# The maximum stage of an attention kernel: two heads a load in 16-row transfers, whole query blocks as units in two 2-bank buffers

## The chip, the cores and the metric

The program runs on one core of one Trainium2 chip. The metric is the time of one execution in device microseconds. A core has five engines that work side by side and meet at semaphores: the tensor engine (PE, with PEld for its weight loads), VectorE (DVE), ScalarE (ACT), GpSimd (POOL) and SyncE (SP), which here only issues DMAs. PSUM, where products land, has 8 banks of 512 fp32 columns on each of 128 partitions.

## The reference

Input x is (4, 2048, 256), H = 16 heads of dh = 16. The output is x plus a causal attention plus a gated layer with 4-bit quantised operands, both on the normalised x:

```python
xn = layernorm(x)
qkv = xn @ Wqkv.T
q, k, v = split into heads of 16
dots = einsum('bhid,bhjd->bhij', q, k) * dh ** -0.5
dots = where(causal_mask, -inf, dots)
attn = softmax(dots)
out = x + (attn @ v) @ Wout.T + bout + fp4_gated_layer(xn)
```

## The kernel before

Four stages follow each other. The weights are prepared; then x is normalised and projected, and q and k go to DRAM, each as a sum of `PARTS` = 3 bf16 parts (`dram["q"]`, `dram["k"]`, a row of T = 2048 tokens for each part and dimension). Then comes the *maximum stage*, `shift_phase`, which this change is about: it finds for each query the largest allowed score, so that the main stage can subtract it before the exponential. The main stage computes the scores again, the probabilities, the values and the gated layer.

The maximum stage goes through B = 4 batches and 2 rounds of `MAX_HEADS` = 8 heads each, so 8 rounds and 64 heads. It needs only maxima, so it folds the keys in halves: of 128 keys, the first 64 (call their scores a) and the next 64 (b). The larger of both is a + relu(b - a). The tensor engine computes b - a into `DIFF` with one product, whose operands stack q parts and their negatives (`q_diff`) on parts of k shifted by 64 tokens and unshifted (`k_st`), and a into `S` with a second product of `q_st` on the same `k_st`. ScalarE writes relu(`DIFF`) to `excess` (line 730). VectorE adds `S` and `excess` and reduces over the columns with a maximum (line 751, one instruction that runs as a reduction and a short read of the accumulator). At the diagonal, a second small product of an identity and `future` adds -1e30 where keys lie ahead (line 686).

A *unit* is one query block i of 128 rows with up to `MAX_KEYS` = 1024 of its (i + 1) x 128 keys, so up to 512 folded columns: 24 units a head, 10 of them with 512 columns and two each with 64, 128, ... 448. Blocks 8 to 15 have two units; the second writes `second_max`, joined with `row_max` at the round's end (line 755). The order pairs a large unit with a small one. `DIFF` and `S` have `MAX_BUFS` = 4 buffers of one bank each, `excess` has 8.

The order on the tensor engine is written out: for each unit u of the round first the differences of u + `MAX_LEAD` (2), then the scores of u. Differences wait until ScalarE has read the unit that had the buffer 4 before, scores until VectorE has reduced the unit 4 before. At a head's first unit, the differences also wait for its load (`stack_ld`) and for GpSimd (`q_negated`), which makes the negative q rows from those that were loaded to `q_st` (line 639).

The loads have two buffers, for even and odd heads. SP waits until VectorE signals at the last unit of a head that its stacks are free (`stack_free`, line 750), and issues the head after next: 8 DMAs of `load_head` (line 547). `MAX_Q` and `MAX_K` give each DMA a first row and the parts it brings. Two parts, or one part twice, are one DMA of 2 x 16 rows with the 2 as its outermost dimension.

At a round's end the tensor engine turns the 128 x 128 maxima (line 719) into the last `DIFF` buffer, ScalarE and VectorE make two bf16 parts of it (lines 734, 758), and GpSimd stores them. The next round's product into that buffer waits for `part1`.

Of the kernel before, what the change touches and what calls it, by code (L numbers as in the profile page):

```python
# [14 lines left out]
P = 128  # L15
# [523 lines left out]
def load_head(eng, dst, src, runs, h, first, tokens, sem):  # L539

    for row, parts in runs:
        n = len(parts)
        if parts[0] == parts[-1]:
            rows = src[parts[0], bass.ds(h * DH, DH), bass.ds(first, tokens)].unsqueeze(0).to_broadcast([n, DH, tokens])
        else:
            rows = src[parts[0]:parts[-1] + 1, bass.ds(h * DH, DH), bass.ds(first, tokens)]
        eng.dma_start(dst[row:row + n * DH, 0:tokens], rows).then_inc(sem, 16)


MAX_KEYS = 1024  # L550
MAX_BUFS = 4
MAX_EXCESS = 8
MAX_LEAD = 2
# [3 lines left out]
def max_units():  # L557

    units = []
    for i in range(NKB):  # L560
        for k0 in range(0, (i + 1) * P, MAX_KEYS):
            units.append((i, k0, min(MAX_KEYS, (i + 1) * P - k0), k0 > 0))
    units.sort(key=lambda unit: -unit[2])
    half = len(units) // 2
    return [unit for pair in zip(units[:half], units[:half - 1:-1]) for unit in pair]


def shift_phase(nc, once, loop_sems, ident, dram):
# [9 lines left out]
    split = MAX_KEYS // P  # L578
    primed = []
    sem = loop_sems(primed)  # L580
    with ExitStack() as ctx:
# [11 lines left out]
        row_max, second_max = sb("m_row_max", [P, MAX_HEADS, NKB]), sb("m_second_max", [P, MAX_HEADS, NKB - split])  # L593
# [9 lines left out]
        joined, turned, part0, part1, stored, shift_st = (  # L603
            sem("m_joined"), sem("m_turned"), sem("m_part0"), sem("m_part1"), sem("m_stored"), once("m_st"))
        aside = once("m_aside")
        rounds = H // MAX_HEADS
        per_round = MAX_HEADS // 2
        head_dmas = len(MAX_Q) + 2 * len(MAX_K)
# [4 lines left out]
        def heads_before(n, h):  # L613

            return n * per_round + h // 2

        round_units = [(h, *unit) for h in range(MAX_HEADS) for unit in units]

        def uses(n, u, bufs):

            return n * (len(round_units) // bufs) + u // bufs + 1

        @block.gpsimd
        def _(pool):
# [10 lines left out]
            def negate(n, h):  # L635
                p = h % 2
                pool.wait_ge(q_ld[p], heads_before(n, h) * (16 * len(MAX_Q)) + 16 * len(MAX_Q) + PRIMED)
                pool.wait_ge(stack_free[p], heads_before(n, h) + PRIMED)
                pool.tensor_tensor(q_diff[p][rows, :], zero[rows, 0:1].to_broadcast([MAX_ROWS, T]), q_st[p][rows, :],  # L639
                                   ALU.subtract).then_inc(q_negated[p], 1)  # L640
# [10 lines left out]
            for h in range(2):  # L651
                negate(0, h)
            with pool.Fori(0, B * rounds - 1) as n:
                for h in range(2, MAX_HEADS):
                    negate(n, h)
                for h in range(2):
                    negate(n + 1, h)
                store(n)
            for h in range(2, MAX_HEADS):
                negate(B * rounds - 1, h)  # L660
            store(B * rounds - 1)

        @block.sync
        def _(sp):
            with sp.Fori(0, B) as b:
                with sp.Fori(0, rounds) as r:
                    n = b * rounds + r
                    for h in range(MAX_HEADS):
                        p = h % 2
                        sp.wait_ge(zeroed[p], 3)  # L670
                        sp.wait_ge(stack_free[p], heads_before(n, h) + PRIMED)
                        head = r * MAX_HEADS + h
                        load_head(sp, q_st[p][MAX_SECOND:P, :], dram["q"], MAX_Q, head, b * T, T, q_ld[p])
                        load_head(sp, q_diff[p], dram["q"], MAX_Q, head, b * T, T, stack_ld[p])

                        load_head(sp, k_st[p], dram["k"], MAX_K, head, b * T + PAIR, T - PAIR, stack_ld[p])
                        load_head(sp, k_st[p][MAX_SECOND:P, :], dram["k"], MAX_K, head, b * T, T, stack_ld[p])

        @block.tensor
        def _(pe):  # L680
            def product(out, q, h, i, k0, keys, mask):

                of = k_st[h % 2][:, k0:k0 + 2 * keys].rearrange("r (n k) -> r n k", k=P)[:, :, 0:PAIR]
                ins = pe.matmul(out[:, 0:keys], q[:, i * P:(i + 1) * P], of, start=True, stop=mask is None)  # L684
                if mask is not None:
                    ins = pe.matmul(out[:, keys - PAIR:keys], ident_bf[:, :], mask, start=False, stop=True)  # L686
                return ins

            def differences(n, u):
                h, i, k0, keys, _ = round_units[u]  # L690
                if u % len(units) == 0:
# [16 lines left out]
            with pe.Fori(0, B) as b:  # L708
                with pe.Fori(0, rounds) as r:
# [3 lines left out]
                    for u in range(len(round_units)):  # L713
                        if u + MAX_LEAD < len(round_units):
                            differences(n, u + MAX_LEAD)
# [679 lines left out]
```

## Time and profile before

| | |
|---|---|
| median of 3 runs | 3051.47 us (3048.34 to 3060.48) |
| profiled execution, first to last instruction | 3047.1 us |
| busy: PE, DVE, ACT, POOL | 2621.8, 1949.4, 2030.3, 694.1 us |
| maximum stage, first product to last part | 251.47 to about 1257 us |
| granted clock, share of DMA engines busy, 250 to 500 us | 0.83, 0.18 |
| VectorE busy, ScalarE busy, 250 to 500 us | 181.03, 159.65 us |

Times are microseconds of one profiled execution, counted from its first instruction. Durations overlap at their ends, because engines are pipelined: a product's record holds the time until its last column has landed. PEclk is the granted tensor clock as a share of 2.4 GHz. DMA share is the mean busy share of 16 DMA engines. "[4.31 <-DMA m_k<-s_k]" reads: the engine stood still for 4.31 us, and this transfer ended it; "issue" is rest that nothing in the profile accounts for.

### The profile page before, as it was taken

The numbers are of one execution on the slowest core, as the hardware profiler recorded it, in microseconds if no ns is written. First come the engines' busy times: TensorE is split into PE (matmuls) and PEld (weight loads), VectorE is DVE, ScalarE is ACT, GpSimd is POOL, SyncE is SP. The second block draws the span as 40 slices with busy tenths as digits, with TensorE's granted clock in tenths as the row PEclk, the third lists the DMA queues.
The fourth block names the chain that finished last, engine by engine and source line by source line (L and its number), as shares of the span: only waits on it lengthen the run. The fifth ranks groups of instructions, "written<-read, shape, count | busy, mean of one in ns | idle before, by whom it ended". The sixth has DMA issues, their size and how long they took to land.

```text
span 3047.1 us, 60898 instructions
## 1 busy us (share of the span) xinstructions
PE 2621.8 (86%) x18236; PEld 1350.3 (44%) x18236; DVE 1949.4 (64%) x5533; ACT 2030.3 (67%) x3510; POOL 694.1 (23%) x510
## 2 busy tenths in 40 slices
PE   2995777777777777599999999999999999999999
PEld 2872333333333333244444544444544444544445
DVE  6986677776777767455656456665556565555665
ACT  1655566665666666387777577777577777677775
POOL 3652212222122222221121121121122111111121
PEclk9997788887888888799999999999999999999999
DMA  2772211121111121322023122113212203302200
GB/s 74 256 255 59 55 47 50 51 53 53 47 50 50 53 53 48 80 43 43 22 37 75 46 37 47 35 28 66 61 28 42 43 22 63 73 22 38 48 21 31
DMA packets 115564, 175.52 MB, mean 58 GB/s; under 512 B 23344, under 2 KB 91696, under 8 KB 114736
## 3 DMA queue, kind: packets, MB, share of 16 engines
q1 hardware_dynamic: 95856, 147.32, 20.2%
q10 hardware_dynamic: 16576, 15.73, 1.9%
q0 software_dynamic: 2816, 8.91, 1.1%
q8 instruction: 118, 1.93, 0.3%
q14 instruction: 198, 1.62, 0.2%
HBM read 129.37 MB, written 42.53 MB: 56 GB/s over the span
## 4 chain that ended last, share of the span: by engine, by line
PE 49%; ACT 4%; issue 3%; DMA 1%; SPq 1%; DVE 0%; ACTq 0%; POOL 0%; DVEq 0%; POOLq 0%
PE O L925 15%; PE S L909 14%; PE F L945 9%; PE F L985 5%; ACT probs L1054 4%; PE F L975 2%; PE S L996 2%; PE S L912 2%; SPq L528 1%; DMA y<-in_L_attn_x_dram 1%; PE F L938 1%; DMA q_st<-s_shift 0%; ACTq L1049 0%; DVE o_turned L1260 0%; DVE ht_lo L1248 0%
## 5 line engine op out<-in xcount | busy, mean ns | idle before, releaser
L1054 ACT ACTIVATE probs<-S 128x1024 f32<-128x1024 f32 (+3 forms) x1280 | 1075.1, 897 | 215.6 <-PE S L909 78.0
L751 DVE CUSTOM_DVE_ANT_0 m_excess<-m_S,m_excess 128x512 f32<-128x512 f32 (+7 forms) x1536 | 718.0, 531 | 285.5 <-PE m_S L686 217.3
L730 ACT ACTIVATE m_excess<-m_DIFF 128x512 f32<-128x512 f32 (+7 forms) x1536 | 635.5, 477 | 367.4 <-PE m_DIFF L686 256.1
L684 PE MATMUL m_DIFF<-m_k,m_q_diff 128*128 128x512 bf16 (+7 forms) x1536 | 540.1, 360 | 269.4 <-DMA m_k<-s_k 242.4
L909 PE MATMUL S<-q_st,k_st 128*128 128x512 bf16 (+3 forms) x2560 | 648.4, 351 | 66.1 <-DMA q_st<-s_shift 28.8
L925 PE MATMUL O<-probs,v_sb 128*32 128x512 f32 (+3 forms) x5120 | 603.3, 543 | 2.1 <-POOL v_sb L1131 2.1
L684 PE MATMUL m_S<-m_k,m_q 128*128 128x512 bf16 (+7 forms) x1536 | 539.7, 363 | 6.0 <-DVE m_second_max L751 2.0
L639 POOL TENSOR_TENSOR m_q_diff<-m_zero,m_q 48x2048 bf16<-48x2048 bf16 x64 | 230.4, 3599 | 763.9 <-DMA m_q<-s_q 755.6
L909 PEld LDWEIGHTS S<-q_st,k_st 128*128 128x128 bf16 x2560 | 213.5, 98 | 409.6 <-ACT probs L1054 236.0
L684 PEld LDWEIGHTS m_DIFF<-m_k,m_q_diff 128*128 128x128 bf16 x1536 | 169.9, 111 | 381.4 <-issue 324.9
L684 PEld LDWEIGHTS m_S<-m_k,m_q 128*128 128x128 bf16 x1536 | 165.3, 108 | 168.9 <-DVE m_row_max L751 126.7
L1248 DVE TENSOR_TENSOR ht_lo<-F,ht_hi 128x512 fp32r<-128x512 f32 (+1 forms) x128 | 71.1, 558 | 231.1 <-ACT ht_hi L1069 231.1
L686 PE MATMUL m_S<-m_future,m_ident 128*128 128x64 bf16 x1024 | 212.8, 209 | 0.0
L686 PE MATMUL m_DIFF<-m_future,m_ident 128*128 128x64 bf16 x1024 | 210.6, 207 | 0.0
L912 PE MATMUL S<-future,ident_bf 128*128 128x128 bf16 x1024 | 195.2, 221 | 0.0
L925 PEld LDWEIGHTS O<-probs,v_sb 128*32 128x32 f32 x5120 | 100.9, 108 | 212.3 <-issue 205.1
L1114 POOL TENSOR_TENSOR h_norm<-gated,h_rscale 128x704 f32<-128x704 f32 x64 | 88.9, 1390 | 438.0 <-DVE h_rscale L1190 438.0
L1099 POOL TENSOR_TENSOR x_norm<-xn,x_rscale 128x256 f32<-128x256 f32 x64 | 48.3, 755 | 559.8 <-DVE x_rscale L1190 559.8
L1223 DVE TENSOR_SCALAR tanh<-tanh 128x352 int32<-128x352 int32 x128 | 69.7, 545 | 161.9 <-ACT decay L1064 161.7
L686 PEld LDWEIGHTS m_DIFF<-m_future,m_ident 128*128 128x128 bf16 x1024 | 109.5, 107 | 76.2 <-issue 28.1
L1254 DVE TENSOR_TENSOR y<-F,y 128x256 f32<-128x256 f32 x64 | 27.1, 424 | 176.1 <-PE F L985 176.1
L1120 POOL TENSOR_TENSOR h_fp<-h_norm,h_scale 128x704 f32<-128x704 f32 x64 | 88.9, 1389 | 189.8 <-DVE h_norm L1200 189.8
(163 smaller groups left out, 4130.7 us busy)
## 6 DMA issues: line engine op xcount, KB each, us to landing
k_st<-s_k SPq DMA_DIRECT2D x96, 256.0 KB, 8.7
q_st<-s_q SPq DMA_DIRECT2D x384, 64.0 KB
s_q<-a_part SPq DMA_DIRECT2D x48, 256.0 KB, 3.0
s_k<-a_part SPq DMA_DIRECT2D x48, 256.0 KB, 2.2
a_x<-in_L_attn_x_dram POOLq DMA_DIRECT2D x16, 512.0 KB, 4.8
s_v<-a_v SPq DMA_DIRECT2D x16, 512.0 KB, 2.9
m_q<-s_q SPq DMA_DIRECT2D x64, 128.0 KB
m_q_diff<-s_q SPq DMA_DIRECT2D x64, 128.0 KB
```

Of the source, the lines that this page charges most:

```text
L639: pool.tensor_tensor(q_diff[p][rows, :], zero[rows, 0:1].to_broadcast([MAX_ROWS, T]), q_st[p][rows, :], ALU.subtract).then_inc(q_negated[p ...
L684: ins = pe.matmul(out[:, 0:keys], q[:, i * P:(i + 1) * P], of, start=True, stop=mask is None)
L686: ins = pe.matmul(out[:, keys - PAIR:keys], ident_bf[:, :], mask, start=False, stop=True)
L730: act.activation(excess[u % MAX_EXCESS][:, 0:keys // 2], DIFF[u % MAX_BUFS][:, 0:keys // 2], ACT.Relu) \
L751: dve.tensor_tensor_reduce(larger, S[u % MAX_BUFS][:, 0:keys // 2], larger, 1.0, -3e38, ALU.add, ALU.max, column).then_inc(reduced[u % MAX ...
L909: ins = pe.matmul(S[half][:, s % 2, 0:st.width], k_st[p][:, s, st.j * P:(st.j + 1) * P], q_st[st.c % 2][:, s, st.skip:QC], start=True, sto ...
L912: ins = pe.matmul(S[half][:, s % 2, 0:P], ident_bf[:, :], future[:, :], start=False, stop=True)
L925: ins = pe.matmul(o[s * SLOT:(s + 1) * SLOT, st.skip:QC], v_sb[st.hg % 2][:, st.j, s * SLOT:(s + 1) * SLOT], probs[s // 2][st.n % 2][:, s ...
L945: ins = pe.matmul(F[f][:, 0:ICH], m[:, kk * P:(kk + 1) * P], w[:, kk, ch * ICH:(ch + 1) * ICH], start=k == 0, stop=k == len(terms) - 1)
L985: ins = pe.matmul(F[1][:, 0:D], h[:, m * P:(m + 1) * P], w[:, m, :], start=k == 0, stop=k == len(terms) - 1)
L1054: act.activation(probs[half][st.n % 2][:, :, 0:st.width], S[half][:, :, 0:st.width], ACT.Exp, scale=SCALE).then_inc(exped[half], 1)
L1114: pool.tensor_tensor(fp4_blocks(h_norm[:, :]), fp4_blocks(gated[n % 2][:, :]), per_block(h_rscale[:, :], hb), ALU.mult).then_inc(h_normed, 1)
```

## The change

A load brings two heads (`MAX_LOAD`) into stacks of [128, 2, T]. The helper `load_head` goes; `load_stack`, which the main stage already uses, issues one DMA for each part: 16 rows, in each of them two heads of T tokens. That makes 12 DMAs of 128 KB (or 124) for two heads. A unit is a whole query block, up to 2048 keys and 1024 folded columns: 16 units a head, two matmuls each from block 8 on, and no join. Heads go through the blocks in alternating order, 15 to 0 and 0 to 15. `DIFF` and `S` have two buffers of two banks, `excess` four of twice the size, and the lead is one unit. GpSimd negates two heads at once.

```diff
-MAX_Q, MAX_K = ((0, (0, 1)), (2 * DH, (0,))), ((0, (0, 0)), (2 * DH, (1,)))
+MAX_Q, MAX_K = (0, 1, 0), (0, 0, 1)
...
+MAX_LOAD = 2
...
-MAX_KEYS = 1024
-MAX_BUFS = 4
-MAX_EXCESS = 8
-MAX_LEAD = 2
+MAX_KEYS = 2048
+MAX_BUFS = 2
+MAX_EXCESS = 4
+MAX_LEAD = 1
+BANK = 512
...
 def max_units():
 
-    units = []
-    for i in range(NKB):
-        for k0 in range(0, (i + 1) * P, MAX_KEYS):
-            units.append((i, k0, min(MAX_KEYS, (i + 1) * P - k0), k0 > 0))
-    units.sort(key=lambda unit: -unit[2])
-    half = len(units) // 2
-    return [unit for pair in zip(units[:half], units[:half - 1:-1]) for unit in pair]
+    return [(h, i if h % 2 else NKB - 1 - i) for h in range(MAX_HEADS) for i in range(NKB)]
...
-        q_diff, q_st, k_st = two("m_q_diff", [P, T], BF16), two("m_q", [P, T], BF16), two("m_k", [P, T], BF16)
+        q_diff, q_st, k_st = (two("m_q_diff", [P, MAX_LOAD, T], BF16), two("m_q", [P, MAX_LOAD, T], BF16),
+                              two("m_k", [P, MAX_LOAD, T], BF16))
...
+                pool.tensor_tensor(q_diff[p][rows, :, :], zero[rows, 0:1].unsqueeze(2).to_broadcast([MAX_ROWS, MAX_LOAD, T]),
+                                   q_st[p][rows, :, :], ALU.subtract).then_inc(q_negated[p], 1)
...
+                        load_stack(sp, q_st[p][MAX_SECOND:P, :, :], dram["q"], MAX_Q, head, MAX_LOAD, bass.ds(b * T, T), q_ld[p])
+                        load_stack(sp, k_st[p][:, :, 0:T - PAIR], dram["k"], MAX_K, head, MAX_LOAD, bass.ds(b * T + PAIR, T - PAIR),
+                                   stack_ld[p])
+                        load_stack(sp, k_st[p][MAX_SECOND:P, :, :], dram["k"], MAX_K, head, MAX_LOAD, bass.ds(b * T, T), stack_ld[p])
+                        load_stack(sp, q_diff[p], dram["q"], MAX_Q, head, MAX_LOAD, bass.ds(b * T, T), stack_ld[p])
...
+            def product(out, q, h, i, mask):
+
+                width = (i + 1) * PAIR
+                for at in range(0, width, BANK):
+                    end = min(at + BANK, width)
+                    of = k_st[h // MAX_LOAD % 2][:, h % MAX_LOAD, 2 * at:2 * end].rearrange("r (n k) -> r n k", k=P)[:, :, 0:PAIR]
+                    pe.matmul(out[:, at:end], q[:, h % MAX_LOAD, i * P:(i + 1) * P], of, start=True, stop=end < width)
+                return pe.matmul(out[:, width - PAIR:width], ident_bf[:, :], mask, start=False, stop=True)
...
-                    pe.wait_ge(joined, n + 1 + PRIMED)
+                    for buf in range(MAX_EXCESS):
+                        pe.wait_ge(reduced[buf], uses(n, len(units) - 1, MAX_EXCESS) + PRIMED)
...
-                    dve.tensor_tensor(row_max[:, :, split:NKB], row_max[:, :, split:NKB], second_max[:, :, :],
-                                      ALU.max).then_inc(joined, 1)
```

The helper that both stages then use stands unchanged at line 525:

```python
def load_stack(eng, dst, src, order, h, heads, tokens, sem):
    for at, k in enumerate(order):
        eng.dma_start(dst[at * DH:(at + 1) * DH, :, :],
                      src[k, bass.ds(h * DH, heads * DH), tokens].rearrange("(h d) t -> d h t", d=DH)).then_inc(sem, 16)
```

## Rows read from the trace of the kernel before

**Rows 1.** The page's first line
```profile
span 3047.1 us, 60898 instructions
```

**Rows 2.** The waits in 252 to 1257: us in total, times, longest
```profile
PE m_DIFF L684 <- DMA m_k<-s_k: 242.4, 55, 27.2
DVE m_excess L751 <- PE m_S L686: 217.3, 96, 13.6
...
ACT m_excess L730 <- issue: 39.0, 7, 6.1
```

**Rows 3.** Instructions by line and shape, 230 to 1340, mean ns
```profile
L751 DVE CUSTOM_DVE_ANT_0 m_excess<-m_S,m_excess 128x512 f32<-128x512 f32 x640 | 440.0, 687 | 94.7 <-ACT m_excess L730 42.2 <-PE m_S L686 26.6 <-PE m_S L684 24.1
L730 ACT ACTIVATE m_excess<-m_DIFF 128x512 f32<-128x512 f32 x640 | 385.5, 602 | 361.7 <-PE m_DIFF L686 256.1 <-PE m_DIFF L684 62.6 <-issue 39.0
L684 PE MATMUL m_DIFF<-m_k,m_q_diff 128*128 128x512 bf16 x640 | 294.8, 461 | 269.4 <-DMA m_k<-s_k 242.4 <-ACT m_excess L730 26.6 <-issue 0.4
L639 POOL TENSOR_TENSOR m_q_diff<-m_zero,m_q 48x2048 bf16<-48x2048 bf16 x64 | 230.4, 3599 | 763.9 <-DMA m_q<-s_q 755.6 <-issue 8.3
...
L730 ACT ACTIVATE m_excess<-m_DIFF 128x64 f32<-128x64 f32 x128 | 28.4, 222 | 0.0
L751 DVE CUSTOM_DVE_ANT_0 m_excess<-m_S,m_excess 128x64 f32<-128x64 f32 x128 | 28.2, 220 | 0.0
```

**Rows 4.** A head's end in order of time: start, us
```profile
594.37 1.11 SPq L547 DMA_DIRECT2D m_q<-s_q  x2
...
608.82 0.61 PE L684 MATMUL m_DIFF<-m_k,m_q_diff 128*128 128x512 bf16 x1 [4.31 <-DMA m_k<-s_k]
...
610.12 0.62 DVE L751 CUSTOM_DVE_ANT_0 m_excess<-m_S,m_excess 128x448 f32<-128x448 f32 x1 [3.99 <-PE m_S L686]
...
610.75 1.13 SPq L547 DMA_DIRECT2D m_q<-s_q  x2
```

**Rows 5.** A stretch of that load: busy us (x), PEclk, DMA share, GB/s
```profile
602.00:608.00 6.00, 2.49 (x21) 1.20 (x19) 4.13 (x18) 2.76 (x6) 1.67 (x1) 1.00 0.12 47
```

**Rows 6.** The main stage's first load: its issue, and a stretch of it
```profile
1263.60 2.74 SPq L528 DMA_DIRECT2D k_st<-s_k  x6
...
1271.00:1273.00 2.00, 0.00 (x0) 0.00 (x0) 0.00 (x0) 0.00 (x0) 0.00 (x0) 0.50 1.03 123
```

**Rows 7.** In order of time, a round's end, VectorE and ScalarE
```profile
622.61 0.08 DVE L751 DVE_READ_ACCUMULATOR2_ANT m_row_max<- 128x1 f32 x1
...
628.98 2.16 ACT L730 ACTIVATE m_excess<-m_DIFF 128x512 f32<-128x512 f32 x6 [5.15 <-issue]
...
629.76 0.69 DVE L751 CUSTOM_DVE_ANT_0 m_excess<-m_S,m_excess 128x512 f32<-128x512 f32 x1 [5.61 <-ACT m_excess L730]
```

**Rows 8.** In order of time, reductions and the product behind one
```profile
601.68 0.08 DVE L751 DVE_READ_ACCUMULATOR2_ANT m_row_max<- 128x1 f32 x1
...
601.82 0.10 PEld L684 LDWEIGHTS m_S<-m_k,m_q 128*128 128x128 bf16 x1 [0.26 <-DVE m_row_max L751]
601.82 0.39 PE L684 MATMUL m_S<-m_k,m_q 128*128 128x512 bf16 x1
...
613.04 0.22 DVE L751 CUSTOM_DVE_ANT_0 m_excess<-m_S,m_excess 128x64 f32<-128x64 f32 x1
...
613.19 0.69 DVE L751 CUSTOM_DVE_ANT_0 m_excess<-m_S,m_excess 128x512 f32<-128x512 f32 x1
```

**Rows 9.** In order of time, the stage's start and end
```profile
233.49 0.91 DVE L740 MEMSET m_q_diff<- 128x1024 f32 x1 [9.55 <-PEq L57]
...
251.47 0.61 PE L684 MATMUL m_DIFF<-m_k,m_q_diff 128*128 128x512 bf16 x1 [27.17 <-DMA m_k<-s_k]
...
1256.68 0.29 DVE L758 SCALAR_TENSOR_TENSOR m_part<-m_DIFF,m_part 128x128 bf16<-128x128 f32 x1 [0.81 <-ACT m_part L734]
```

**Rows 10.** Two stretches of 3.4 us, columns as in group 5
```profile
618.80:622.20 3.40, 2.01 (x16) 0.77 (x14) 3.40 (x15) 1.50 (x4) 1.58 (x1) 1.00 0.13 52
629.80:633.20 3.40, 3.40 (x20) 1.73 (x19) 2.79 (x13) 2.76 (x8) 2.76 (x3) 0.62 0.17 63
```

More of the change, by code:

```diff
@@ L602, in shift_phase, with loads_before @@
         scored, reduced = sems("m_scored", MAX_BUFS), sems("m_reduced", MAX_EXCESS)
-        joined, turned, part0, part1, stored, shift_st = (
-            sem("m_joined"), sem("m_turned"), sem("m_part0"), sem("m_part1"), sem("m_stored"), once("m_st"))
+        turned, part0, part1, stored, shift_st = (
+            sem("m_turned"), sem("m_part0"), sem("m_part1"), sem("m_stored"), once("m_st"))
         aside = once("m_aside")
         rounds = H // MAX_HEADS
-        per_round = MAX_HEADS // 2
-        head_dmas = len(MAX_Q) + 2 * len(MAX_K)
+        loads = MAX_HEADS // MAX_LOAD
+        per_load = MAX_LOAD * NKB
+        load_dmas = len(MAX_Q) + 2 * len(MAX_K)
         prime(nc, primed)
         block = ctx.enter_context(nc.Block())
-        def heads_before(n, h):
-            return n * per_round + h // 2
-        round_units = [(h, *unit) for h in range(MAX_HEADS) for unit in units]
+        def loads_before(n, load):
+            return n * (loads // 2) + load // 2
         def uses(n, u, bufs):
-            return n * (len(round_units) // bufs) + u // bufs + 1
+            return n * (len(units) // bufs) + u // bufs + 1
         @block.gpsimd
@@ L650, in _ @@
             pool.wait_ge(consts, 5)
-            for h in range(2):
-                negate(0, h)
+            for load in range(2):
+                negate(0, load)
             with pool.Fori(0, B * rounds - 1) as n:
[L654 to L657, printed above, removed]
+                for load in range(2, loads):
+                    negate(n, load)
+                for load in range(2):
+                    negate(n + 1, load)
                 store(n)
-            for h in range(2, MAX_HEADS):
-                negate(B * rounds - 1, h)
+            for load in range(2, loads):
+                negate(B * rounds - 1, load)
             store(B * rounds - 1)
@@ L667, in _ @@
                     n = b * rounds + r
-                    for h in range(MAX_HEADS):
-                        p = h % 2
+                    for load in range(loads):
+                        p = load % 2
                         sp.wait_ge(zeroed[p], 3)
[L671 to L677, printed above, removed]
+                        sp.wait_ge(stack_free[p], loads_before(n, load) + PRIMED)
+                        head = r * MAX_HEADS + load * MAX_LOAD
+                        load_stack(sp, q_st[p][MAX_SECOND:P, :, :], dram["q"], MAX_Q, head, MAX_LOAD, bass.ds(b * T, T), q_ld[p])
[3 more added lines that the diff above has]
+                        load_stack(sp, q_diff[p], dram["q"], MAX_Q, head, MAX_LOAD, bass.ds(b * T, T), stack_ld[p])
@@ L679, in _ @@
         @block.tensor
         def _(pe):
[L681 to L687, printed above, removed]
-            def differences(n, u):
-                h, i, k0, keys, _ = round_units[u]
-                if u % len(units) == 0:
-                    pe.wait_ge(stack_ld[h % 2], heads_before(n, h) * (16 * head_dmas) + 16 * head_dmas + PRIMED)
-                    pe.wait_ge(q_negated[h % 2], heads_before(n, h) + 1 + PRIMED)
+            def product(out, q, h, i, mask):
[5 more added lines that the diff above has]
+                return pe.matmul(out[:, width - PAIR:width], ident_bf[:, :], mask, start=False, stop=True)
```

59 lines of the change are left out of this document (25 added, 34 removed).

## The prediction

> **What bounds the kernel now.** I first took the span from the page [rows 1], then the chain of waits inside the maximum stage [rows 2], to see who stands still and for whom. The tensor engine's first product of a head waits 242.4 us for `m_k` to land, and VectorE waits 217.3 us for products; nothing of that size is a wait of the tensor engine for VectorE. So the stage is not paced by arithmetic. The instructions by line and shape [rows 3] say what arithmetic would cost, and the instructions in order of time around one head's end [rows 4] show the circle that paces it:
>
> - SP issues a head's load at 594.37. The first product that needs it starts at 608.82, after 4.31 us of standing still, so this load took 14.4 us. `MAX_LEAD` puts the next head's first products ahead of the last scores of the head before. So VectorE cannot finish the old head until the load is there: it takes the last units at 610.12, frees the stack, and SP issues the next load at 610.75. One turn is 610.75 - 594.37 = 16.4 us, of which 14.4 is the load.
> - The stage lasts from 251.47 to about 1257.0, the end of the last `m_part` [rows 9], so 1005.5 us or 15.7 us a head for 64 heads.
>
> Why is a load of 762 KB (192 rows of 4 KB, some of them 64 columns shorter) so slow? In the stretch 602 to 608 the DMA share is 0.12, two of 16 engines, at 47 GB/s [rows 5]. Four of a head's eight transfers have two copies or two parts as their outermost dimension (about 508 KB); at 47 GB/s those alone take 10.8 us.
>
> The trace's reading can stand alone. The Trainium skill (DMA: Bandwidth & Descriptors, Rules for kernel authors) says the same of such a shape: an outermost dimension of c below 16 confines a transfer to at most c engines. By that rule the trace's 0.12 is the cause and 16-row transfers cure it.
>
> **The change part by part.**
>
> *The load.* Two heads come in 12 transfers of 16 rows, 1.52 MB. The nearest row is the main stage's load of k and q in the same shape (its q rows are shorter): there all 16 engines are busy (share 1.03), and they move only 123 GB/s [rows 6]. So 16 rows on 16 engines are 2.6 times as fast as now, not 8 times. 1.52 MB at 123 GB/s is 12.4 us, with about 1.5 us before the first byte 14 us for two heads. The negation doubles from 3.6 us [rows 3] to 7.2 us, but q comes first: 3 of 12 transfers land about 4.5 us after the issue, so it ends at about 12 us, beside the rest of the load. The 12 issues cost SP 6 to 7 us at about 0.6 us each [rows 4]; nothing but loads is behind them on its queue. What hides all this is the arithmetic of the other buffer's two heads, at least 2 x 10.4 us (below). The slack is about 7 us. So the load leaves the path, 4 us of stall a head go, and the next limit is arithmetic.
>
> *VectorE, now the bound.* A 512-column reduction begins 0.61 us before the next one, a 64-column one 0.15 us (613.04 to 613.19, [rows 8]; 0.687 and 0.220 us of record less 0.08 of overlap). The slope is (687 - 220) / 448 = 1.042 ns a column, the fixed part 0.083 us. A head has 8704 columns either way: 64 x (1 + ... + 16). Before: 9.07 + 24 x 0.083 = 11.1 us. After: 9.07 + 16 x 0.083 = 10.4 us. No row has 1024 columns on this line; I take the straight line.
>
> *ScalarE.* The same from 602 and 222 ns [rows 3]: 0.848 ns a column and, with overlap, about 0.095 us fixed: 8704 x 0.848 ns + 16 x 0.095 = 8.9 us a head, below VectorE.
>
> *The tensor engine.* The products are the same in number and columns: a 1024-column unit still needs two matmuls, each block a mask of 64. That is 2 x (8704 + 1024) = 19456 columns, 8.1 us at 2.4 GHz and 16.2 us at 1.2 GHz. So the clock decides which engine is the bound, and I come back to it.
>
> *Two buffers in place of four, lead 1 in place of 2, no pairing of large with small.* This is the added wait. Scores of unit u wait for the reduction of u - 2, and behind them on the tensor engine's queue stand the differences of u + 2, for which ScalarE waits. From the end of a reduction to the next product is 0.06 us (601.76 to 601.82, [rows 8]); the product takes w / 2.4 GHz plus 0.03 for the mask; its last column lands 0.17 us later (0.39 us of record against 0.213 of streaming); then about 0.06 us to VectorE. That is 0.32 + 0.417w us, w in thousands of columns. VectorE meanwhile works on unit u - 1, with 1.042w + 0.083 from a start that lies 0.08 before. What it stands still is 0.32 - 0.63w: nothing from about 500 columns on, and for 64 to 448 columns together 7 x 0.32 - 0.63 x 1.79 = 1.1 us a head. At large units it has 0.3 us to spare. From below the gap is 0 (VectorE at 10.4 us), from above about twice this, as the differences in between can add to it. I take 1.1: a head is 11.5 us, and 64 are 736 us.
>
> *The round's end.* VectorE's last reduction ends at 622.69, its next begins at 629.76 [rows 7]. Most of it is ScalarE, which stands 5.15 us for nothing that the profile shows, after its loop turns; 39.0 us in 7 turns, 5.6 each [rows 2]. The loop is kept, so I keep 5.6; the join goes, and the first unit's activation grows by 0.43. The turned maximum now lies in the second of two buffers, so the second product waits for `part1`; that is done within 1.5 us and lies under ScalarE's stall. I take 7.4 us a turn, 52 us for 7. After such a rest the clock is low: 0.62 granted in 629.8 to 633.2 [rows 10]. At 1.2 GHz a 1024-column unit is 2 x 1088 / 1.2 = 1.81 us of products against 1.15 of reduction; over some 4 us that costs 1.5 us, eight times: 12 us.
>
> *The start.* The memsets double: three of 0.91 us [rows 9] come before the first load, so it goes out 2.8 us later; it takes about as long as the first one did. First product at about 254, first reduction at about 256.
>
> *Sum.* 256 + 736 + 52 + 12 + 1.1 for the last turn = 1057, against 1257.0: 200 us less. What follows is untouched. The profiled span was 3047.1 us, the median of the runs 3051.5, that is 4.4 more; against the median the forecast is **2851 us**, 6.6% faster.
>
> **The clock, where a rule speaks against this.** In 618.8 to 622.2 the tensor engine was busy 2.01 of 3.40 us with a full granted clock, waiting for VectorE again and again [rows 10]; where it was low, it stood behind a rest. After the change the engine streams 8.1 of 11.5 us. Where two heads meet, around the smallest blocks, eight units of 64 to 256 columns stream 3584 columns, 1.5 us in about 3. I keep the full clock.
>
> The Trainium skill (TensorE: Matmul & The Clock Gate, on cycling through PSUM buffers) warns that an engine which idles briefly between groups of matmuls can swing between both clocks. That would be the first rival. By the rule it is about 2910 us, by the row 2851.
>
> **The rivals.**
>
> 1. *The clock falls where the small blocks meet* and is low for some 5 us of every two heads. Cost as above, 5 x (1 - 1.15 / 1.81) = 1.8 us, times 32: 58 us, **2910 us**. For it: nowhere before were there 12 short units in a row. Against: 618.8 to 622.2. Chance 0.12.
> 2. *The loads do not get faster*, because something other than the two engines sets their pace. Two heads then take 2 x 14.4 plus about 1.5 us, 32 turns 970 us and the last rounds' rests partly on top: **about 3035 us**. Against: the share of 0.12, and 123 GB/s in the other shape. Chance 0.03.
> 3. *The slow side: the clock stays at 1.2 GHz*, since products in two deep buffers always pause. Then 64 x 16.2 = 1037, plus 52 and the rest, about 1095 for the stage: **about 3145 us**. It decides from a head of 14.7 us on, (1005 - 64) / 64. Against: at half clock the products would fill the engine, and in 629.8 to 633.2, busy 3.40 of 3.40 us, it was given more than half [rows 10]. Chance 0.04.
> 4. *Every unit pays the 0.32 us*, not only small ones, because the in-order queue ties the two buffers together: 16 x 0.32 = 5.1, a head of 15.5 us, **about 3105 us**. Against: the spare 0.3 us at large units. Chance 0.03.
>
> **How the numbers follow.** The forecast has 0.78. Its own range is 2780 (no gaps) to 2910 (gaps twice as long, or a longer rest at the round's end). With rival 1 inside, 2795 to 2925 holds about 8 in 10. A measurement of this kernel tells about 0.5% (15 us) from no change. Faster by more: 0.78 + 0.12, and the better half of rival 2, 0.91. Within: 0.02. Slower: 0.07.
>
> **What the profile after would show.** Right: no wait of the tensor engine for `m_k` except the first; DMA share well over 0.12 while a load runs, and a load over within 15 us; VectorE with a 1024-column form of about 1.22 us, its 64-column reductions 0.3 us apart, large ones back to back; heads in pairs of 23 us; a granted clock over 0.9 in the stage; ScalarE's 5 us at each round's end. Wrong: a granted clock near 0.8 or less, gaps between large reductions, or loads that still end after the arithmetic.

## The result, and the profile after

The changed kernel takes 2851.88 us, the median of 4 runs (2851.32 to 2852.8); the kernel before, on the same chip, 3051.41 us (3048.34 to 3060.48). The ratio is 0.9346, with a 95% interval of 0.933 to 0.9362: 6.5% faster. The forecast was 2851 us. That it fits to 1 us is luck in part: six of its terms were off by 3 to 15 us, and they cancel.

The page of the kernel after. The span answers to [rows 1]; the next two rows are 40 slices of 71 us; the last two are DMA queues with packets, MB and share of 16 engines.

```profile
span 2850.6 us, 58193 instructions
...
PEclk7997999999999997999999999999999999999999
DMA  2775444433444325122031221231220222220200
...
q8 instruction: 118, 1.93, 0.3%
q14 instruction: 145, 1.19, 0.2%
```

Slices 4 to 15 are the maximum stage. The granted clock fills nine tenths in nearly all of them.

The waits of the kernel after in 245 to 1075 (us in total, times, longest), which answer to [rows 2]:

```profile
PEld m_S L671 <- DVE m_row_max L737: 251.8, 830, 4.3
ACT m_excess L716 <- PE m_DIFF L672: 151.5, 397, 29.6
DVE m_excess L737 <- issue: 38.5, 7, 6.3
PE m_DIFF L671 <- DMA m_q_diff<-s_q: 30.0, 1, 30.0
DVE m_excess L737 <- PE m_S L672: 22.8, 57, 11.5
```

The 242.4 us for `m_k` are gone: the only wait of the tensor engine for a load is the first. What it waits for now is VectorE, 830 times. VectorE is the bound. Beside its wait for the first product it has one long rest at each of seven round ends, and small ones for products.

By line and shape in 230 to 1080 (count, total, mean ns), which answers to [rows 3]:

```profile
L623 POOL TENSOR_TENSOR m_q_diff<-m_zero,m_q 48x4096 bf16<-48x4096 bf16 x32 | 224.4, 7012 | 561.4 <-DMA m_q<-s_q 550.0 <-issue 11.3
L737 DVE CUSTOM_DVE_ANT_0 m_excess<-m_S,m_excess 128x1024 f32<-128x1024 f32 x64 | 76.3, 1220 | 50.0 <-issue 38.5 <-PE m_S L672 11.5
L716 ACT ACTIVATE m_excess<-m_DIFF 128x1024 f32<-128x1024 f32 x64 | 65.6, 1026 | 38.2 <-PE m_DIFF L672 37.2
```

The reduction of 1024 columns takes 1220 ns, the forecast's 1.22 us. The negation takes 7.0 us, forecast 7.2.

SP's queue in order of time: the first DMAs of four loads in a row. Between two of them VectorE reduces two heads.

```profile
282.35 1.28 SPq L528 DMA_DIRECT2D m_q<-s_q  x3
...
305.84 1.29 SPq L528 DMA_DIRECT2D m_q<-s_q  x3
...
329.26 1.29 SPq L528 DMA_DIRECT2D m_q<-s_q  x3
...
352.77 1.38 SPq L528 DMA_DIRECT2D m_q<-s_q  x3
```

Two heads take 23.47 us ((352.77 - 282.35) / 3), a head 11.74; before it was 15.7. The first of these periods, cut at 296.3, and three stretches from a round's end on (busy us and count of PE, PEld, DVE, ACT, POOL, then PEclk, DMA share, GB/s, as in [rows 5]):

```profile
282.30:296.30 14.00, 12.09 (x96) 5.82 (x94) 13.19 (x42) 10.67 (x21) 7.01 (x1) 1.00 0.77 114
296.30:305.80 9.50, 9.50 (x68) 4.51 (x66) 9.20 (x25) 9.13 (x13) 0.00 (x0) 1.00 0.01 2
...
356.60:361.30 4.70, 2.68 (x12) 1.05 (x11) 1.30 (x3) 2.66 (x4) 3.15 (x1) 0.75 1.04 138
...
361.30:364.30 3.00, 2.86 (x14) 1.39 (x15) 2.81 (x5) 1.14 (x2) 3.00 (x1) 0.68 1.01 130
...
365.00:440.00 75.00, 68.62 (x511) 32.80 (x508) 71.35 (x204) 62.63 (x102) 19.98 (x6) 0.99 0.42 60
```

The cut at 296.3 is a generous one. The load dies away before 295, and the last thing it brings, the negation, ends at 294.6:

```profile
287.60 7.01 POOL L623 TENSOR_TENSOR m_q_diff<-m_zero,m_q 48x4096 bf16<-48x4096 bf16 x1 [20.64 <-DMA m_q<-s_q]
...
294.30:294.80 0.50, 0.42 (x7) 0.28 (x8) 0.36 (x3) 0.37 (x2) 0.31 (x1) 1.00 0.05 8
```

So a load with its negation takes 12.3 us (282.35 to 294.6) and leaves 11 us of the period free. The granted clock is full, 2.4 GHz, away from the round ends; behind this one it is 0.75, then 0.68. It falls behind all seven, while VectorE stands or right after; only at the fourth is it full again by the first reduction, at 666.3.

The start, a round's end, and the end of the stage in order of time, which answer to [rows 7, 9]:

```profile
236.03 1.76 DVE L726 MEMSET m_q_diff<- 128x2048 f32 x1 [9.47 <-DVEq L57]
...
242.52 1.37 SPq L528 DMA_DIRECT2D m_q<-s_q  x3
...
256.93 1.03 PE L671 MATMUL m_DIFF<-m_k,m_q_diff 128*128 128x512 bf16 x2 [30.02 <-DMA m_q_diff<-s_q]
...
260.00 1.22 DVE L737 CUSTOM_DVE_ANT_0 m_excess<-m_S,m_excess 128x1024 f32<-128x1024 f32 x1 [11.51 <-PE m_S L672]
...
354.75 0.29 DVE L740 SCALAR_TENSOR_TENSOR m_part<-m_DIFF,m_part 128x128 bf16<-128x128 f32 x1 [0.87 <-ACT m_part L720]
...
355.59 1.89 ACT L716 ACTIVATE m_excess<-m_DIFF 128x1024 f32<-128x1024 f32 x2 [0.87 <-PE m_DIFF L672]
...
355.92 1.04 PE L671 MATMUL m_S<-m_k,m_q 128*128 128x512 bf16 x2
...
360.00 1.23 DVE L737 CUSTOM_DVE_ANT_0 m_excess<-m_S,m_excess 128x1024 f32<-128x1024 f32 x1 [4.95 <-issue]
...
1066.23 0.29 DVE L740 SCALAR_TENSOR_TENSOR m_part<-m_DIFF,m_part 128x128 bf16<-128x128 f32 x1 [0.94 <-ACT m_part L720]
```

ScalarE, which stood 5.15 us in [rows 7], starts 0.9 us after its part is written. The scores of the first unit are there by 357.0, the end of the x2 group that began at 355.92. It is VectorE that starts only at 360.00, after 4.95 us that the profile gives to nothing; the first 2 of them go by before the scores are there, the other 3 do not.

### The profile page after: what moved, and what is told of

The parts are those of the page before. It is cut to its first block, busy times and chain, and to the rows that moved or that the text cites. A ratio compares the mean times of both kernels' runs of the same rounds, so it can differ in the third digit from the quotient of the medians.

```text
span 2850.6 us, 58193 instructions
## 1 busy us (share of the span) xinstructions
PE 2590.0 (91%) x18236; PEld 1317.7 (46%) x18236; DVE 1948.0 (68%) x4501; ACT 2025.6 (71%) x2998; POOL 688.1 (24%) x478
## 3 DMA queue, kind: packets, MB, share of 16 engines
q1 hardware_dynamic: 97392, 147.33, 27.5%
q8 instruction: 118, 1.93, 0.3%
q14 instruction: 145, 1.19, 0.2%
## 4 chain that ended last, share of the span: by engine, by line
PE 53%; ACT 4%; issue 3%; DMA 1%; SPq 0%; DVE 0%; ACTq 0%; POOL 0%; DVEq 0%; POOLq 0%
PE O L907 17%; PE S L891 15%; PE F L927 10%; PE F L967 5%; ACT probs L1036 4%; PE F L957 2%; PE S L894 2%; PE S L978 2%; PE F L920 1%; DMA y<-in_L_attn_x_dram 1%; SPq L528 0%; ACTq L1031 0%; DVE ht_lo L1230 0%; DVE y L1264 0%; ACT ht_hi L1051 0%
## 5 line engine op out<-in xcount | busy, mean ns | idle before, releaser
L737 DVE CUSTOM_DVE_ANT_0 m_excess<-m_S,m_excess 128x1024 f32<-128x1024 f32 (+15 forms) x1024 | 712.6, 723 | 92.0 <-issue 38.5
L716 ACT ACTIVATE m_excess<-m_DIFF 128x1024 f32<-128x1024 f32 (+15 forms) x1024 | 630.4, 625 | 184.4 <-PE m_DIFF L672 151.5
L671 PE MATMUL m_S<-m_k,m_q 128*128 128x512 bf16 (+7 forms) x1536 | 424.2, 331 | 81.8 <-DVE m_row_max L737 32.7
L671 PE MATMUL m_DIFF<-m_k,m_q_diff 128*128 128x512 bf16 (+7 forms) x1536 | 413.1, 325 | 35.9 <-DMA m_q_diff<-s_q 30.0
L623 POOL TENSOR_TENSOR m_q_diff<-m_zero,m_q 48x4096 bf16<-48x4096 bf16 x32 | 224.4, 7012 | 561.4 <-DMA m_q<-s_q 550.0
L671 PEld LDWEIGHTS m_S<-m_k,m_q 128*128 128x128 bf16 x1536 | 109.4, 98 | 272.0 <-DVE m_row_max L737 251.8
L672 PE MATMUL m_DIFF<-m_future,m_ident 128*128 128x64 bf16 x1024 | 199.2, 195 | 0.0
L672 PE MATMUL m_S<-m_future,m_ident 128*128 128x64 bf16 x1024 | 199.2, 195 | 0.0
L671 PEld LDWEIGHTS m_DIFF<-m_k,m_q_diff 128*128 128x128 bf16 x1536 | 116.7, 99 | 81.7 <-issue 38.6
L1043 ACT ACTIVATE decay<-F 128x352 f32<-128x352 f32 x128 | 59.5, 465 | 107.5 <-PE F L927 107.5
```

Source lines behind the costliest of these rows:

```text
L623: pool.tensor_tensor(q_diff[p][rows, :, :], zero[rows, 0:1].unsqueeze(2).to_broadcast([MAX_ROWS, MAX_LOAD, T]), q_st[p][rows, :, :], ALU.s ...
L671: pe.matmul(out[:, at:end], q[:, h % MAX_LOAD, i * P:(i + 1) * P], of, start=True, stop=end < width)
L672: return pe.matmul(out[:, width - PAIR:width], ident_bf[:, :], mask, start=False, stop=True)
L716: act.activation(excess[u % MAX_EXCESS][:, 0:width], DIFF[u % MAX_BUFS][:, 0:width], ACT.Relu) \
L737: dve.tensor_tensor_reduce(larger, S[u % MAX_BUFS][:, 0:width], larger, 1.0, -3e38, ALU.add, ALU.max, row_max[:, h, i:i + 1]).then_inc(red ...
```

## The experiments

All ratios are to the kernel before, on the same chip, with their 95% intervals. The variants ran on three chips, where the kernel before took 3051.47, 3053.79 and 3051.51 us. What follows the maximum stage has the same code in all kernels and took 1784 to 1794 us, for a cause that I don't know. So a difference of medians under 10 us means little by itself, and where it matters the stage's own times are given.

| kernel | median, us | ratio |
|---|---|---|
| the change | 2851.88 | 0.9346 (0.933 to 0.9362) |
| e1_load_alone | 2813.42 | 0.9215 (0.9195 to 0.9235) |
| e2_units_alone | 3008.13 | 0.9843 (0.982 to 0.9867) |
| e3_paired_order | 3023.57 | 0.9904 (0.9883 to 0.9925) |
| e4_load_twice | 2943.98 | 0.9647 (0.9623 to 0.967) |
| e5_one_head_16row | 2786.64 | 0.9123 (0.9107 to 0.914) |
| e6_rounds_unrolled | 2847.84 | 0.9324 (0.9308 to 0.9341) |
| e8_small_paired | 2793.33 | 0.9147 (0.913 to 0.9163) |
| e9_small_paired_unrolled | 2783.91 | 0.9117 (0.91 to 0.9133) |
| e10_load_held | 2829.14 | 0.9275 (0.9262 to 0.9287) |
| e11_one_head_paired | 2760.54 | 0.905 (0.9038 to 0.9063) |
| e12_all | 2769.77 | 0.9076 (0.9064 to 0.9089) |

**The two parts apart.** The kernel before with the load of the change, its units, four buffers and lead of two kept:

```diff
-MAX_Q, MAX_K = ((0, (0, 1)), (2 * DH, (0,))), ((0, (0, 0)), (2 * DH, (1,)))
+MAX_Q, MAX_K = (0, 1, 0), (0, 0, 1)
+MAX_LOAD = 2
...
-                        load_head(sp, q_st[p][MAX_SECOND:P, :], dram["q"], MAX_Q, head, b * T, T, q_ld[p])
+                        load_stack(sp, q_st[p][MAX_SECOND:P, :, :], dram["q"], MAX_Q, head, MAX_LOAD, bass.ds(b * T, T), q_ld[p])
```

> The kernel before with the load part of the change alone: two heads a load in 12 transfers of 16 rows; units, buffers, order and lead as before. Theory (two engines paced the load, the units matter little): the load leaves the path and VectorE sets the pace without gaps, since four buffers and large units paired with small ones hide the latency: 24 units, 11.1 us a head against 11.74 measured after the whole change. That is 64 x 0.64 = 41 us less than the changed kernel, about 2815 us. Rival (a good part of the gain comes from whole blocks as units): slower than the changed kernel, 2880 us or more.

Measured 2813.42 us, as expected: 238 us from the load alone, more than the whole change brings. A head takes 10.96 us (loads of two heads go out at 299.28, 321.12 and 343.13). ScalarE keeps its rest at the round's end. The waits of this kernel in 245 to 1030:

```profile
PEld m_S L687 <- DVE m_row_max L755: 180.3, 607, 1.0
...
ACT m_excess L734 <- issue: 36.4, 7, 5.8
```

The other part alone, the changed kernel with one head a load and the transfers of before:

```diff
-MAX_LOAD = 2
+MAX_LOAD = 1
...
-                        load_stack(sp, q_st[p][MAX_SECOND:P, :, :], dram["q"], MAX_Q, head, MAX_LOAD, bass.ds(b * T, T), q_ld[p])
+                        load_head(sp, q_st[p][MAX_SECOND:P, 0, :], dram["q"], MAX_Q, head, b * T, T, q_ld[p])
```

> The changed kernel with the loads of before: one head a load, eight transfers, four of them with two copies or parts outermost; whole blocks as units, two buffers, alternating order and lead 1 as in the change. Theory: the circle of load (14.4 us) and what lies between its landing and the next free stack (1.5 to 2 us) sets the pace again, about 16.2 us a head: 3050 us, within 20. Rival (whole blocks bring a good part): about 2950 us.

Measured 3008.13 us, 42 less than expected and outside the 20 that it gave. Two turns of this kernel in order of time, the first where heads meet at their small blocks, the second at their large ones:

```profile
282.76 1.11 SPq L548 DMA_DIRECT2D m_q<-s_q  x2
...
297.75 0.23 PE L681 MATMUL m_DIFF<-m_k,m_q_diff 128*128 128x64 bf16 x1 [2.82 <-DMA m_k<-s_k]
298.49 0.66 SPq L548 DMA_DIRECT2D m_q<-s_q  x1
...
312.28 1.03 PE L681 MATMUL m_DIFF<-m_k,m_q_diff 128*128 128x512 bf16 x2 [3.81 <-DMA m_k<-s_k]
...
314.67 1.11 SPq L548 DMA_DIRECT2D m_q<-s_q  x2
```

The load still paces. Only one unit of the old head is held back by the lead of one. Where heads meet at the small blocks it is a short one, and from the first product to the next load 0.74 us pass, against 610.75 - 608.82 = 1.93 in [rows 4]; where they meet at the large ones it is 2.39. Over the stage the mean is 1.5 us, before 1.9. That is about half of the gain: in the profiled run the eight rounds are together 14 us shorter than before (935.0 against 949.4). The gaps between rounds are 17 us shorter (35.5 against 52.8), which the expectation left as they were. So the units part takes 43 us off where the load is the bound, and with the new load it costs 38.5 us (2851.88 - 2813.42).

**What the units cost: order and banks.** The changed kernel with a large block beside a small one, in the same two buffers:

```diff
-    return [(h, i if h % 2 else NKB - 1 - i) for h in range(MAX_HEADS) for i in range(NKB)]
+    return [(h, i) for h in range(MAX_HEADS) for k in range(NKB // 2) for i in (NKB - 1 - k, k)]
```

> The changed kernel with the blocks in the order 15, 0, 14, 1, ... in every head, in place of 15 to 0 and 0 to 15. Theory (VectorE stands still where what it does meanwhile is shorter than the product of the next unit and its latency, 0.40 + 0.417 w(next) - 1.042 w(now) - 0.083 us): 2.8 us a head in place of 1.1, so 64 x 1.7 = 109 us more, about 2960 us. Rival (the order of blocks does not matter with two buffers, the gaps are a fixed cost of each unit): no change, about 2852 us.

Measured 3023.57 us: the direction was right, the size short by 64. Two of its views, a large unit behind a small one, and a whole period of two heads:

```profile
286.67 0.22 DVE L737 CUSTOM_DVE_ANT_0 m_excess<-m_S,m_excess 128x64 f32<-128x64 f32 x1
...
286.81 0.58 PE L671 MATMUL m_S<-m_k,m_q 128*128 128x512 bf16 x2 [0.78 <-DVE m_row_max L737]
...
287.22 0.19 PE L672 MATMUL m_S<-m_future,m_ident 128*128 128x64 bf16 x1
287.63 1.16 DVE L737 CUSTOM_DVE_ANT_0 m_excess<-m_S,m_excess 128x960 f32<-128x960 f32 x1 [0.74 <-PE m_S L672]
```

```profile
284.00:313.00 29.00, 19.63 (x162) 10.17 (x160) 22.02 (x65) 18.22 (x32) 7.01 (x1) 1.00 0.36 56
```

The product begins 0.06 us after the reduction of two units before ends (286.75 to 286.81); that agrees with [rows 8]. But the mask's record ends at 287.41, and VectorE starts 0.22 us later, where the prediction had 0.06. With 0.16 more at each of 8 large units, the expected 2.8 us of gaps a head become 4.1. The trace has 8.0 us for two heads, and a head is 29.07 / 2 = 14.5 us. The alternating order is therefore what makes two buffers bearable; it is worth 172 us here. The tensor engine is busy 19.63 of 29 us, pauses before each large unit, and is granted the full clock. The Trainium skill (TensorE: Matmul & The Clock Gate, A second HAM failure mode: psum-queue depth-cycling) tells of a kernel whose clock swings between its two levels when such short pauses come often. Here and in the kernel after the granted clock is low only behind the start and in the first 15 us behind a round's end; elsewhere in the stage no stretch of 4 us has less than 0.98.

Then the small blocks two by two, one in each bank of a buffer, so that 12 units make a head:

```diff
+    blocks = [((i, 0),) for i in range(NKB - 1, half - 1, -1)] + [((half - 1 - k, 0), (k, BANK)) for k in range(half // 2)]
+    return [(h, unit) for h in range(MAX_HEADS) for unit in (blocks[::-1] if h % 2 else blocks)]
...
+                        for i, at in blocks:
+                            end = at + (i + 1) * PAIR
+                            larger = excess[u % MAX_EXCESS][:, at:end]
+                            ins = dve.tensor_tensor_reduce(larger, S[u % MAX_BUFS][:, at:end], larger, 1.0, -3e38, ALU.add, ALU.max,
+                                                           row_max[:, h, i:i + 1])
+                        ins.then_inc(reduced[u % MAX_EXCESS], 1)
```

> The changed kernel with blocks 0 to 7 two by two in one unit, one in each bank of a buffer (7 with 0, 6 with 1, ...): 12 units a head, same instructions on ScalarE and VectorE. Theory (VectorE stands still for 1.3 us a head only at small units, where its work on one unit is shorter than the next product and its latency): every unit now has at least 0.74 us of reductions against 0.7 of product and latency, the gaps go to 0.2 us or less, so 64 x 1.1 = 70 us less, about 2780 us. Rival (the gaps are a fixed price of two buffers, paid at every unit or at the head's ends): 2820 us or more.

Measured 2793.33 us, 58.5 less than the change where 70 were expected. A head is 10.7 to 10.8 us and the gaps of two heads fall from 2.7 us to between 0.6 and 1.0. This shows that the gaps between small units were most of what a head costs above its reductions.

**The load's share.** The changed kernel with each transfer issued a second time into spare stacks:

```diff
+        again = [two(f"m_again{k}", [P, MAX_LOAD, T], BF16) for k in range(3)]
...
+                        load_stack(sp, again[2][p], dram["q"], MAX_Q, head, MAX_LOAD, bass.ds(b * T, T), stack_ld[p])
```

> The changed kernel with every load issued twice, the second into spare stacks, all of it waited for: 24 transfers, 3.05 MB for two heads. Theory (16-row transfers move about 125 GB/s whatever is done, and the changed kernel's loads have some 9 us of slack in 23.45): a load takes about 26 us, with 1.5 us of turn-round 27.5 us for two heads, 32 x 4 = 130 us more, about 2980 us. Rival (a load is mostly latency and issue time, not rate): 14 us plus 5.6 us of issues stay below 23 us, no change, about 2855 us.

Measured 2943.98 us, 36 less than expected. A load in order of time:

```profile
291.98 1.28 SPq L528 DMA_DIRECT2D m_q<-s_q  x3
...
316.24 0.60 PE L677 MATMUL m_DIFF<-m_k,m_q_diff 128*128 128x512 bf16 x2 [2.21 <-DMA m_q_diff<-s_q]
...
318.06 0.32 SPq L528 DMA_DIRECT2D m_q<-s_q  x1
```

Twice the bytes take 24.3 us, twice the 12.3 us of the load above, and come back on the path, with a period of 26.1 us. The expectation had 26 and 27.5, from a rate of 125 GB/s; it is higher (139 GB/s in 296 to 302). So in the changed kernel the load has slack, as forecast, and more of it.

One head a load, but 16 rows a transfer, in the units of before (e1 with one number changed):

```diff
-MAX_LOAD = 2
+MAX_LOAD = 1
```

> The kernel before with 16-row transfers and still one head a load (12 transfers of 64 KB): units, buffers, order and lead as before. Theory (the outermost dimension alone is the cause): 762 KB at 125 GB/s and 1.5 us are 8 us, below the 11 us of a head's arithmetic, so it is as fast as the variant with two heads a load, 2813 us within 10. Rival (a load must be large, or be issued two heads ahead, to be hidden): 2850 us or more.

Measured 2786.64 us, 27 less than e1_load_alone and outside the 10 of the expectation. Joining two heads in a load brings nothing here, only the 16 rows do; the joining costs 27 us. The gaps between rounds are 35.0 us in all, where e1 has 55.7 (ScalarE's rests in them 20.2 against 36.4). The first reduction comes 7.4 us earlier too (248.27 against 255.66), with half the memsets and half the first load before it.

**The round's end.** The loop over rounds, written out on SP, the tensor engine, ScalarE and VectorE:

```diff
-with dve.Fori(0, rounds) as r:
+for r in range(rounds):
```

> The changed kernel with the two rounds of a batch written out in place of the inner loop, on all engines but GpSimd: 3 loop turns in place of 7. Theory (the rest of 5.5 us that VectorE has at each round's end belongs to its loop turn): at 4 of 7 round ends VectorE waits for the first product only and starts some 3 us earlier, about 12 us less, 2840 us. Rival (the rest belongs to the end of the round, wherever the loop is): no change, 2852 us.

Measured 2847.84 us, a gain of 4 where 12 were expected; the intervals of both ratios overlap, so the total doesn't show a gain by itself. Two round ends of this kernel, VectorE and the tensor engine, the second one where the loop over batches turns:

```profile
355.21 1.23 DVE L737 CUSTOM_DVE_ANT_0 m_excess<-m_S,m_excess 128x1024 f32<-128x1024 f32 x1 [2.05 <-PE m_S L672]
...
457.13 1.03 PE L671 MATMUL m_DIFF<-m_k,m_q_diff 128*128 128x512 bf16 x2 [5.55 <-issue]
...
460.20 1.23 DVE L737 CUSTOM_DVE_ANT_0 m_excess<-m_S,m_excess 128x1024 f32<-128x1024 f32 x1 [7.98 <-PE m_S L672]
```

At the four ends without a turn VectorE stands 1.3 to 2.0 us between its part and its first reduction, and waits for products. So of the 5 to 6 us of the kernel after some 3 to 4 belong to the loop's turn, and the rest to the products. At the three ends where the batch loop turns it is 7.9 to 8.0, because there the tensor engine itself rests first. Together 29.9 us, against 38.5 in the kernel after. The stage ends at 1056.1 instead of 1066.5, but 2.2 us of that lie before the first reduction, where the code is the same, and what follows the stage took 7 us longer in this run.

The other way keeps the loop and takes the transfers away from its turn: SP holds the second load of each round until the round's first unit is reduced.

```diff
                         sp.wait_ge(stack_free[p], loads_before(n, load) + PRIMED)
+                        if load == 1:
+                            sp.wait_ge(reduced[0], uses(n, 0, MAX_EXCESS) + PRIMED)
```

> The changed kernel; at a round's end SP holds the load that becomes free there until the next round's first unit is reduced (one more wait on its queue). Theory (the rest of 5.5 us at a loop turn is the fetch of instructions, which queues behind the 1.5 MB of loads on the DMA engines; it was 2.9 us with small loads and 6.8 us with doubled ones): with the engines free at the turn VectorE's rest falls to about 3 us, the round end shortens by some 2.5 us, 7 x 2.5 = 17 us less, about 2835 us; the held load is 14 us long and still lands before it is needed. Rival (the rest is a fixed price of the turn, and its size went by the engine that had it): no change or, as the load comes later, a little slower, 2852 to 2860 us.

Measured 2829.14 us, 22.7 less than the change, by one added wait. VectorE's waits in 245 to 1050:

```profile
DVE m_excess L739 <- PE m_S L674: 30.2, 41, 11.2
DVE m_excess L739 <- issue: 9.3, 3, 3.3
```

The profile calls three of the seven stands "issue" and puts four to products. In order of time each is 3.0 to 3.3 us, where the kernel after has 5.0 to 6.3: 22.1 us against 38.5. A second gain is the clock. This kernel, a stretch behind the same round's end:

```profile
357.20:360.20 3.00, 2.65 (x18) 1.31 (x18) 3.00 (x7) 2.35 (x4) 0.00 (x0) 1.00 0.56 117
```

The clock falls here as well, to 0.5 to 0.7 between 353.5 and 357.5, mostly while VectorE stands anyway; then it is full, and VectorE is busy 3.00 of 3.00 us. In the kernel after it falls a second time, to 0.5 between 362.5 and 365.5, behind a rest of the tensor engine of 2.02 us (it waits for VectorE's late start), and then VectorE is the one that waits. In this kernel that rest is 0.16 us. All eight rounds together are 6.7 us shorter than in the kernel after, and the gaps between them 16.2 us. While VectorE stands the DMA share is 0.01, in the kernel after 1.02 to 1.07: with the transfers held, a rest at the turn is 2.3 us shorter.

**Together.** e8 with the loop written out:

```diff
-with dve.Fori(0, rounds) as r:
+for r in range(rounds):
```

> Both of the last two edits: small blocks two by two in a unit, and the rounds written out. Theory (they are independent): the sum of the two, about 2768 us. Rival (one of them takes what the other gives): within 5 us of the variant with small blocks paired.

2783.91 us, 9.4 less than e8 where 12 were expected (and 16 above the 2768 that both expectations gave together). e8 with one head a load:

```diff
-MAX_LOAD = 2
+MAX_LOAD = 1
```

> The changed kernel with small blocks two by two in a unit and one head a load, in 12 transfers of 16 rows and 64 KB. Theory (smaller loads start the stage earlier, by about 7 us, and shorten the seven turns by 2.5 us each, whatever the units are): 2793 less 25, about 2768 us. Rival (with two 2-bank buffers and a lead of one unit there is less time for a load than in the variant with four buffers, about 9 us for a load of 8 plus the negation, so stalls come back at the heads' ends): 2790 us or more.

2760.54 us, the fastest of all: 9.5% under the kernel before and 3.2% under the change (2760.54 / 2851.88). Against e8 it gains 11.9 us at the start (first reduction at 247.62 instead of 259.50), 15 at the seven round ends, where VectorE stands 3.1 to 3.9 us, in e8 4.9 to 6.3, and 6 inside the rounds. Then the same, written out as in e9:

```diff
-with dve.Fori(0, rounds) as r:
+for r in range(rounds):
```

> As the last, with the two rounds of a batch written out (3 loop turns in place of 7). Theory: about 8 us less than that variant, 2760 us. Rival (with small loads a turn is short enough to be hidden behind the round's own latency): the same within 3 us.

2769.77 us: 9 slower, a miss. Only 3 us of it are in the stage, which ends at 974.6 instead of 971.5. VectorE stands 1.7 to 2.2 us at the four ends without a turn, but 6.5 to 6.7 at the three where the batch loop turns, 27.9 us against 24.5. The other 7 us are in what follows the stage (1794.0 against 1787.0), whose code is the same. All three kernels with the loop written out have it long, 1791 to 1794 us, but e2, e5 and e8 reach 1791 without, and I don't know why.

## Why the prediction was right, and where it was not

- **The load leaves the path: right.** The tensor engine waits for one load, the first. A load took 12.3 us with its negation, where 14 was forecast: the rate was 143 to 150 GB/s while it ran, not 123. The slack is 11 us, forecast 7. e4 and e1 show it from both sides. Rival 2 is out, and by e1 the transfers' shape was worth more than the whole change.
- **VectorE becomes the bound: right.** Its reductions cost what the straight line gave, 10.4 us a head.
- **The gap term, 1.1 us a head: two errors that nearly cancel.** Measured are 11.74 - 10.4 = 1.3. First, the end of a product to VectorE was taken as 0.06 us, which no row showed; it is 0.22. Second, each unit below 500 columns was given its full loop, as if every one had a wait to itself. The kernel after, where the small blocks meet:

```profile
271.69 0.23 DVE L737 CUSTOM_DVE_ANT_0 m_excess<-m_S,m_excess 128x64 f32<-128x64 f32 x1 [0.17 <-PE m_S L672]
...
271.99 0.26 PE L671 MATMUL m_S<-m_k,m_q 128*128 128x192 bf16 x1
...
272.06 0.29 DVE L737 CUSTOM_DVE_ANT_0 m_excess<-m_S,m_excess 128x128 f32<-128x128 f32 x1
272.08 0.19 PE L672 MATMUL m_S<-m_future,m_ident 128*128 128x64 bf16 x1
...
272.49 0.36 DVE L737 CUSTOM_DVE_ANT_0 m_excess<-m_S,m_excess 128x192 f32<-128x192 f32 x1
```

  The unit of 192 goes round from the end of the reduction that frees its buffer, 271.93, to its own start, 272.49. That is 0.56 us, or 0.48 + 0.417 x 0.192. In that time VectorE has reduced the unit of 128 between, and that one had waited as well. When both neighbours wait, one loop serves two units, and a unit stands still for half of 0.48 - 0.63w us, w in thousands of columns. This runs on to 704 columns: 11 units, (11 x 0.48 - 0.63 x 4.224) / 2 = 1.31 us a head. The trace has 2.7 us of gaps for two heads. Large units pay nothing (360.00, 361.15 with the next one, behind a record of 1.23), so rival 4 is out.
- **The round's end: the size held, the engine was wrong.** "Most of it is ScalarE" stands in the prediction, with 5.6 us kept for it. In the kernel after it is VectorE, 38.5 us in 7 turns, 5.5 each, of which e6 shows 1.3 to 2.0 to be a wait for products; ScalarE starts after 0.9 us. In e1, where the units are those of before, ScalarE keeps it. Which part of the units moved it no run told apart.
- **The clock: right in kind.** Behind a round's end it is granted 0.75 and 0.68, and in 361.3 to 364.3 the tensor engine is busy 2.86 of 3.00 us, while between 363 and 366.1 VectorE waits 0.2 to 0.3 us before each of three large units. The shortest of the eight rounds, from its first reduction to its last, has 93.9 us (8 x 11.74), and the eight together 7.8 us more than 8 times that. Forecast were 12, 1.5 in each of eight rounds; six of them have it, 0.9 to 1.6 each. The seven gaps between rounds are 46.6 us, forecast 52. Elsewhere the clock is full: rivals 1 and 3 are out.
- **The start: forecast 4 us too early, and 2.5 of them are no error of the change's terms.** The first reduction was forecast at 256 and came at 260.0. In this run the stage's first memset begins at 236.03, before at 233.49 [rows 9], and in e3 and e6, with the same code up to there, at 233.72 and 233.98. The first load went out at 242.52 and needed 14.4 us, as forecast. From the first product to the first reduction there are 3.07 us, where 2 were allowed: the first unit is twice as large, at half clock.
- **What follows the stage: taken as untouched, and it was 6 us shorter.** 2850.6 - 1066.5 = 1784.1 us, before 1790.1. In the other kernels this part was 1785 to 1794, and its code is the same in all. I know no cause.

The stage's end was forecast at 1057 and came at 1066.5: start +4, heads +15 (64 x 0.24), gaps between rounds -5, clock -4. With -6.0 from what follows and -3.1 from a median that lay 1.3 us over the span instead of 4.4, 2851 comes out again. The last two, and 2.5 of the start, are differences between runs that nobody forecast.

## What to carry to other kernels

Of a change with several parts, forecast each alone: here the load was worth 238 us and the units took 38.5 of it back, which one sum over both hides. Inside the load part it was the 16 rows that counted; two heads a load cost 27 us. With two buffers in place of four, write the loop from the end of a consumer's work to its next start with measured handoffs both ways, and ask whether neighbours wait in the same loop; small tiles are best put together in one buffer's banks. A transfer that goes out just when a loop turns can be held by one wait, and that was worth 22.7 us.

## What the runs showed of the hardware

- **A loop's turn was shorter when the transfers were held back from it.** One added wait (e10) took the DMA share at the turn from 1.02 to 1.07 down to 0.01, and VectorE's stand from 5.5 to 3.2 us. Without a turn it is 1.3 to 2.0 us (e6). The longest rest at a turn was 6.8 us with the doubled load (e4), 5.6 before, 5.5 after, 5.2 in e1, 2.9 in e5 with half a load; before, in e1 and in e5 it is ScalarE's. The share alone does not put them in order: before has 5.6 us at a share of 0.32 to 0.54, e5 2.9 at 0.44 to 0.55, and in e2, with the loads of before in flight (0.29 to 0.47), VectorE stands 3.8 us and mostly waits for products at half clock. The page has DMA queues of the kind "instruction", 1.93 and 1.19 MB, so instructions come by DMA as well; that they queue behind the load's packets is argued from this and not shown. The Trainium skill (Runtime: NRT & Kernel Launch, Instruction fetch mechanics) says that a taken branch to a target outside the pages at hand must wait until a DMA has fetched it. The traces agree with such a stall; that it grows with other transfers the page does not say.
- **Sixteen rows fill all engines, but not their rate.** At a share of 1.04 the kernel after moved 138 GB/s, e4 139 at 1.02, [rows 6] 123 at 1.03; in the stage before this one other transfers moved 263 GB/s at a share of 0.79 (142.5 to 213.8 us of the kernel after). The Trainium skill (SBUF — State Buffer, Door 1: The DMA port swizzle) maps 16 partitions in a row to 4 of 16 ports and gives about 109 GB/s as the most that one such transfer can reach. The traces lie somewhat above, with several transfers in flight; no run here had more rows on all 16 engines in this stage, so the cause stays open.
- **Handoffs are not alike.** From a reduction's end to the product that waits for it 0.06 us pass ([rows 8]; e3, 286.75 to 286.81), from the product's end to VectorE 0.22 us (e3, 287.41 to 287.63; kernel after, 272.27 to 272.49).
